# First graph layer of a fused graph and expert kernel: norms' squares summed on VectorE, early roots, and an aggregation that takes TH tile by tile for all banks

## The chip, the cores and the metric

One Trainium2 chip, one core. The metric is the device time of one execution, in microseconds; of several executions the median counts. TensorE is abbreviated PE (PEld for its weight loads), VectorE DVE, ScalarE ACT, GpSimd POOL, the engine that issues the DMAs SP.

## What is computed

Four blocks in a row, each added to its input: a hyperbolic graph convolution network of two layers on 625 nodes with 10,000 edges, a mixture of 8 experts, a plain graph network, and a linear attention block. The change lies in the first block, nearly all of it in its second layer. Cut to what matters:

```python
def gcn_conv(x, W, b, row, col, norm, n):
    h = mobius_matvec(W, x)         # mx = x @ W.T; needs |x| and |mx| of every row
    h = mobius_add(h, expmap0(b))   # needs the rows' dot products with the bias
    t = logmap0(h)                  # needs |h|, then artanh(|h|)
    msg = norm[:, None] * t[row]
    agg = jax.ops.segment_sum(msg, col, num_segments=n)
    return expmap0(agg)             # needs |agg|

def mobius_matvec(W, x):
    mx = x @ W.T
    xn, mxn = jnp.maximum(_norm(x), EPS), jnp.maximum(_norm(mx), EPS)
    res = jnp.tanh(mxn / xn * artanh(xn)) * mx / mxn
    return project(res)

x = x + _L0_gnn_ref(_layernorm(x, axis=-1), edge_index, ...)   # two gcn_conv
x = x + _L0_ffn_ref(_layernorm(x, axis=-1)[None], ...)[0]      # 8 experts, top 2
```

## The kernel before, in words

The 625 rows are five tiles (t = 0 to 4) of 125 partitions and 512 columns. The sum over edges is a matmul with a dense 625 x 625 count matrix, built from one-hot tiles (OHs, OHd) early in the kernel. A product of float32 accuracy is made from three single passes: each operand is split in a high part and a rest (CH and CL for the count matrix, TH and TL for the scaled messages, UH and UL for the aggregated features, W2H and W2L for the weights), and high x high, low x high and high x low are added up in a PSUM bank. PSUM has eight banks, PS[:, 0] to PS[:, 7], of 512 columns each.

Every engine has its own program, in the order in which it is written (`pe_gnn0`, `v_gnn0`, `a_gnn0`, `g_gnn0`, then the `..._moe` ones); engines wait for each other by counters only (`x.of(key)` is waited for, `x.up(key)` is counted up by the instruction that makes it). An engine whose next instruction waits does nothing behind it. The stages around the change, in order of time:

1. Aggregation of layer 0 (`pe_gnn0`, `share`, L914): for each of four feature blocks f and two halves h, a bank PS[2f+h] sums TH[k] x CH[k] over the five tiles k, then TL x CH, then TH x CL. ACT makes TH[k] one after the other (`a_scaled`, L486), DVE makes TL[k] (`v_scaled`, L492).
2. ACT copies the result of each f to UH and squares it to SQ[:, f]; DVE makes UL.
3. Token matmuls of layer 1 (`pe_token_matmul`, L822): twelve matmuls of 512 columns for each row tile t, in bank t. After t = 1 come the input norms: 20 matmuls of one column (4 blocks x 5 row tiles) of SQ with a column of ones, in bank 7 (`ss_mm`, L951).
4. The row step of layer 1: ACT squares each bank with its row sum (`a_rows`, L460, "ssm"), DVE multiplies it with the bias (`v_rows`, L342, "my"). POOL takes the square roots of ten columns at once, five of the input's norms (nu) and five of the product's (nm), when the last is there (L569). Then a chain of small instructions on DVE, five or ten columns wide: "rr" and "rcp" (the norms' reciprocals), "w" (from nu), "arg" (w x nm); Tanh on ACT; some twenty more up to "n2c" (L411); a root on POOL; then x, m, p, a polynomial, Ln on ACT, and the scale S. ACT meanwhile makes TT from the bias, DVE makes M[t] from bank t and TT[t] (`tangent`).
5. Aggregation of layer 1 (L952 to L962): PE waits for "n2c", runs 17 filler matmuls in bank 6 (`pe_busy`, results not used), and then for each row tile t takes 15 matmuls of 512 columns in bank t: CH x TH, CH x TL, CL x TH, five k each. Its waits are for M[t] and, before every k, for TL[k].
6. ACT squares each bank's result (JO), POOL takes the roots, DVE scales and adds into X. PE turns X (`ut_bank`, L1121) and makes the gate's logits; filler before that is in bank 6 (L1514). Routing follows, and then the experts' weight stream: SP loads a weight tile only when the matmuls that used its slot before are done (`w_used`, L1088). The first eight tiles are loaded long before.

## Time and profile before

| | us |
|---|---|
| median of 3 runs | 2160.74 (2158.61 to 2163.36) |
| profiled execution | 2158.04 |
| its span, first to last instruction | 2156.3 |
| TensorE busy in the span | 2096.2 (97%), 13312 matmuls |
| VectorE, ScalarE, GpSimd busy | 1491.4, 1119.2, 869.1 |
| stretch of the trace that the change touches | about 102 to 189 us |

The profile is of one execution. Its times are counted from the first instruction. The granted clock is the share of full speed that TensorE is given: 1.00 is 2.4 GHz, 0.50 is 1.2 GHz, and a value between them means that a window holds some of both. A matmul on float32 data that is not pre-split appears as two records, so the 20 norm matmuls are 40 rows. A window's count includes matmuls that only reach into it.

### The profile page before, as it was taken

To read this page: it belongs to the slowest core of one execution; us is meant where nothing else is said; L and a number is where in the kernel's file an instruction comes from. 1 tells how busy PE (TensorE), PEld (TensorE's weight loads), DVE (VectorE), ACT (ScalarE), POOL (GpSimd) and SP (SyncE) were. 2 spreads that over 40 slices of the span, in tenths; PEclk is the share of its full clock that TensorE was granted. 3 is DMA by queue.
4 is the path that set the end of the run, shared out by engine and by line. 5 is a ranking of instruction groups with operands and counts; after the bars stand their busy time and mean duration, and the time that the engine had idled before them with its cause. 6 is when DMAs were issued, how large, how long until landed. Compare 5 with 4: busy or idle time off the path is not lost.

```text
span 2156.3 us, 36026 instructions
## 1 busy us (share of the span) xinstructions
PE 2096.2 (97%) x13312; PEld 1956.7 (91%) x13312; DVE 1491.4 (69%) x3168; ACT 1119.2 (52%) x2999; POOL 869.1 (40%) x699
## 2 busy tenths in 40 slices
PE   8887999989999999999999999999999999999998
PEld 7766666677789999999999999999999999999997
DVE  8737988665366667767766677677666776776676
ACT  4534667624355455555554555555545555555464
POOL 0000000201165445555554555555545555555461
PEclk9888999999989999999999999999999999999999
DMA  6000899950131111123211111122111112221110
GB/s 215 1 28 11 301 333 332 272 188 1 34 120 63 63 63 63 63 65 107 81 63 63 63 63 63 65 104 83 63 63 63 63 63 66 106 81 63 60 45 24
DMA packets 89161, 201.15 MB, mean 93 GB/s; under 512 B 8196, under 2 KB 12580, under 8 KB 88985
## 3 DMA queue, kind: packets, MB, share of 16 engines
q1 hardware_dynamic: 86746, 196.28, 26.6%
q0 software_dynamic: 2240, 2.57, 0.5%
q8 instruction: 106, 1.74, 0.3%
q14 instruction: 69, 0.57, 0.1%
HBM read 196.31 MB, written 2.51 MB: 92 GB/s over the span
## 4 chain that ended last, share of the span: by engine, by line
PE 91%; DVE 4%; ACT 2%; DMA 1%; POOL 1%; issue 1%; SPq 0%; DVEq 0%; POOLq 0%; ACTq 0%
PE PS L54 82%; PE PS L53 5%; PE PS L57 4%; DMA YH<-y_rows,IH 1%; DMA X<-in_x 0%; DVE SM L107 0%; DVE OHs L68 0%; POOL SM L60 0%; DVE X L60 0%; POOL YL L125 0%; DVE OHd L69 0%; POOL YH L125 0%; ACT EE L88 0%; DVE JU L66 0%; DVE M L75 0%
## 5 line engine op out<-in xcount | busy, mean ns | idle before, releaser
L54 PE MATMUL PS<-ZH,WS 128*128 128x314 f32 x4096 | 946.5, 311 | 0.0
L54 PEld LDWEIGHTS PS<-ZH,WS 128*128 128x128 f32 x4096 | 692.2, 189 | 0.0
L54 PE MATMUL PS<-ZL,WS 128*128 128x314 f32 x2048 | 626.1, 306 | 0.0
L60 DVE TENSOR_TENSOR ACC<-ACC,PS 128x314 f32<-128x314 f32 x1008 | 476.6, 477 | 196.8 <-PE PS L54 186.8
L54 PEld LDWEIGHTS PS<-ZL,WS 128*128 128x128 f32 x2048 | 387.7, 189 | 0.0
L60 POOL TENSOR_TENSOR WS<-RAW,WS 128x512 fp32r<-128x512 f32 x256 | 326.1, 1294 | 117.0 <-ACT WS L88 117.0
L60 POOL TENSOR_TENSOR ZS<-ZS,ZQ 128x628 f32<-128x628 f32 x128 | 198.3, 1549 | 231.0 <-ACT ZQ L88 231.0
L60 POOL TENSOR_TENSOR ML<-MF,MH 128x400 fp32r<-128x400 f32 x124 | 130.7, 1054 | 364.5 <-ACT MH L88 364.5
L88 ACT ACTIVATE ZH<-PS,g1T 128x628 fp32r<-128x628 f32 x128 | 100.4, 785 | 313.8 <-PE PS L54 313.8
L88 ACT ACTIVATE EE<-EE,SM 125x100 f32<-125x100 f32 x640 | 233.0, 376 | 0.1
L88 ACT ACTIVATE MF<-PS 128x400 f32<-128x400 f32 x128 | 64.7, 505 | 315.9 <-PE PS L53 315.9
L75 DVE SCALAR_TENSOR_TENSOR ZL<-PS,g1T,ZH 128x628 fp32r<-128x628 f32 x128 | 111.6, 872 | 119.8 <-ACT ZQ L88 119.8
L60 POOL TENSOR_TENSOR WQ<-RAW,WQ 128x512 fp32r<-128x512 f32 x128 | 167.9, 1312 | 40.1 <-ACT WQ L88 40.1
L60 DVE TENSOR_TENSOR EE<-PS,CB 125x400 f32<-125x400 f32 x160 | 91.9, 575 | 132.3 <-PE PS L54 131.8
L60 DVE TENSOR_TENSOR EE<-EE,SM 125x500 f32<-125x500 f32 x128 | 153.6, 1200 | 4.4
L88 ACT ACTIVATE WS<-RAW 128x512 fp32r<-128x512 f32 x256 | 147.5, 633 | 0.0
L88 ACT ACTIVATE ATH<-PS 100x500 fp32r<-100x500 f32 (+1 forms) x256 | 96.4, 429 | 94.3 <-PE PS L57 94.3
L54 PE MATMUL PS<-MH,XH 128*125 128x400 f32 x640 | 144.2, 347 | 0.0
L54 PE MATMUL PS<-MH,XL 128*125 128x400 f32 x640 | 143.4, 346 | 0.0
L54 PE MATMUL PS<-ML,XH 128*125 128x400 f32 x640 | 142.9, 345 | 0.0
L53 PEld LDWEIGHTS PS<-KCL,WQ 128*128 128x128 f32 x1024 | 130.4, 192 | 2.2 <-issue 2.0
L53 PE MATMUL PS<-KCL,WQ 128*128 128x200 f32 (+1 forms) x1024 | 128.5, 268 | 0.8 <-DVE KCL L60 0.4
(354 smaller groups left out, 3565.3 us busy)
## 6 DMA issues: line engine op xcount, KB each, us to landing
RAW<-in_L_ffn_wz_w SPq DMA_DIRECT2D x66, 1024.0 KB, 5.9
RAW<-in_L_ffn_w SPq DMA_DIRECT2D x64, 1024.0 KB, 6.5
RAW<-in_L_ffn_Wq_w SPq DMA_DIRECT2D x32, 1024.0 KB, 8.6
CB<-c_rows SPq DMA_DIRECT2D x32, 195.3 KB
RAW<-in_L_gnn_W SPq DMA_DIRECT2D x4, 1024.0 KB, 15.9
RAW<-in_L_ffn_Wkv_w SPq DMA_DIRECT2D x4, 1024.0 KB, 15.2
RAW<-in_L_ffn_Wk_T SPq DMA_DIRECT2D x2, 1024.0 KB, 17.6
WB<-w_rows SPq DMA_DIRECT2D x6, 273.4 KB
```

Source lines behind the costliest of these rows:

```text
L53: return self.q.matmul(o, l, r, start=start, stop=stop, skip_group_check=True)
L54: return self.q.matmul(o, l, r, start=start, stop=stop)
L57: return Nothing() if self.q is None else self.q.transpose(o, i, idn)
L60: return Nothing() if self.q is None else self.q.tensor_tensor(out=o, in0=a, in1=b, op=op)
L75: return self.q.scalar_tensor_tensor(out=o, in0=a, scalar=s, in1=b, op0=op0, op1=op1)
L88: return self.q.activation(o, i, f, **kw)
```

## The change

- Aggregation of layer 0, blocks f = 0 and 1: the first pass (TH x CH) runs with k outside; each TH[k] is used for the four banks before the next is waited for. The number of matmuls stays.
- DVE adds SQ[:, 1], SQ[:, 2] and SQ[:, 3] into SQ[:, 0], after the four UL. The norms then take five matmuls instead of 20; they stand behind t = 2 instead of t = 1, and wait for the last sum. DVE copies them out one row tile earlier in its own order.
- POOL takes the roots in two instructions of five columns: nu as soon as it is there, nm behind the last square. DVE makes nu's reciprocal and "w" after "my" of tile 3; behind nm's roots stands "arg" at once, and nm's reciprocal (five columns instead of ten) behind that.
- ACT runs a Ln of one column right behind Tanh, whose result is not used.
- Aggregation of layer 1: the banks are 0, 1, 5, 6, 7 (`ag_bank`). The first pass (CH x TH) runs with k outside and waits for TH[k], not TL[k]; it also waits for M[1] and for the copy of the norms out of bank 7. Then 10 matmuls for each t.
- The gate's and the experts' banks are renumbered to fit (`ut_bank`, the mean term in bank 4, filler in bank 3, the table `free`).

```diff
@@ -361,18 +361,28 @@
                 else:
                     q.wait_ge(*row_a.of(1, "ssm", t))
                 step(q.stt(TT[:, t, :], rows_of_M(t), 1.0, Yk[:, :], ALU.mult, ALU.mult, acc=c["my"][:, t:t + 1]), ("my", t))
+                if k == 1 and t == 3:
+                    q.wait_ge(*row_g.of(1, "nu"))
+                    step(q.ts(ru, nu, EPS, None, ALU.max), "rru")
+                    after_("rru")
+                    step(q.rcp(ru, ru), "rcu")
+                    after_("rcu")
+                    step(q.stt(c["w"], ru, ATN, dis, ALU.mult, ALU.min), "w")
                 yield
             q.wait_ge(*row_g.of(k, "nn"))
-            step(q.ts(c["rr"], c["nn"], EPS, None, ALU.max), "rr")
-            after_("rr")
-            step(q.rcp(c["rr"], c["rr"]), "rcp")
-            after_("rcp")
             if k == 0:
+                step(q.ts(c["rr"], c["nn"], EPS, None, ALU.max), "rr")
+                after_("rr")
+                step(q.rcp(c["rr"], c["rr"]), "rcp")
+                after_("rcp")
                 step(q.ts(c["w"], ru, ATN, 1.0, ALU.mult, ALU.min), "w")
-            else:
-                step(q.stt(c["w"], ru, ATN, dis, ALU.mult, ALU.min), "w")
             after_("w")
             step(q.tt(c["w"], c["w"], nm, ALU.mult), "arg")
+            if k == 1:
+                step(q.ts(rm, nm, EPS, None, ALU.max), "rr")
+                after_("rr")
+                step(q.rcp(rm, rm), "rcp")
+                after_("rcp")
             yield
             q.wait_ge(*row_a.of(k, "r"))
             step(q.ts(c["r"], c["r"], MAXN, None, ALU.min), "r")
@@ -473,6 +483,8 @@
                 yield
             q.wait_ge(*row_v.of(k, "arg"))
             q.act(c["r"], c["w"], ACT.Tanh).then_inc(*row_a.up(k, "r"))
+            if k == 1:
+                q.act(R3["th"][:, 0:1], ones[0:P, 0:1], ACT.Ln).then_inc(*row_a.up("log"))
             yield
             for t in range(T5):
                 q.wait_ge(*row_v.of(k, "be"))
@@ -565,8 +577,9 @@
             q.wait_ge(*dis_v.of("deg"))
             g_power(q, dis, dis, hm[0:P, 0:5], row_g, "dis")
             q.wait_ge(*row_v.of(1, "ssu"))
+            g_power(q, R[1]["nn"][:, 0:5], R[1]["ss"][:, 0:5], hp[0:P, 0:5], row_g, 1, "nu")
             q.wait_ge(*row_a.of(1, "ssm", 4))
-            g_power(q, R[1]["nn"], R[1]["ss"], hp[0:P, 0:10], row_g, 1, "nn")
+            g_power(q, R[1]["nn"][:, 5:10], R[1]["ss"][:, 5:10], hp[0:P, 0:5], row_g, 1, "nn")
             q.wait_ge(*row_v.of(1, "n2c"))
             g_power(q, R[1]["n"], R[1]["n"], hp[0:P, 0:5], row_g, 1, "n")
             q.wait_ge(*row_a.of("out", "ss", 4))
@@ -656,7 +669,7 @@
             next(moe)
             for t in range(T5):
                 q.wait_ge(*ag_done.of(1, t))
-                q.act(JO[:, t, :], PS[0:P, t, :], ACT.Square, acc=R3["ss"][:, t:t + 1]).then_inc(*row_a.up("out", "ss", t))
+                q.act(JO[:, t, :], PS[0:P, ag_bank[t], :], ACT.Square, acc=R3["ss"][:, t:t + 1]).then_inc(*row_a.up("out", "ss", t))
             q.wait_ge(*row_v.of("out", "nd"))
             q.act(R3["th"], R3["nd"], ACT.Tanh).then_inc(*row_a.up("out", "th"))
             q.wait_ge(s_vec, 80)
@@ -789,8 +802,13 @@
             for f in range(4):
                 q.wait_ge(*u2_hi.of("u", f))
                 q.tt(halves(UL[:, f, :]), pair(f), halves(UH[:, f, :]).bitcast(f32), ALU.subtract).then_inc(*u2_lo.up(f))
+            for f in range(1, 4):
+                q.wait_ge(*u2_hi.of("sq", f))
+                if f >= 2:
+                    q.wait_ge(*u2_lo.of("sum", f - 1))
+                q.tt(SQ[:, 0, :], SQ[:, 0, :], SQ[:, f, :], ALU.add).then_inc(*u2_lo.up("sum", f))
             rows = v_rows(q, 1)
-            for t in range(4):
+            for t in range(3):
                 next(rows)
             q.wait_ge(*ss_mm.of())
             q.cp(R[1]["ss"][:, 0:5], PS[0:P, 7, 0:5]).then_inc(*row_v.up(1, "ssu"))
@@ -809,11 +827,13 @@
             q.stt(R3["cc"], R3["th"], MAXN, R3["rn"], ALU.min, ALU.mult).then_inc(*row_v.up("out", "cc"))
             q.wait_ge(*row_v.of("out", "cc"))
             for t in range(T5):
-                q.stt(X[:, t, :], PS[0:P, t, :], R3["cc"][:, t:t + 1], X[:, t, :], ALU.mult, ALU.add).then_inc(*x1_done.up(t))
+                q.stt(X[:, t, :], PS[0:P, ag_bank[t], :], R3["cc"][:, t:t + 1], X[:, t, :], ALU.mult, ALU.add).then_inc(*x1_done.up(t))
             q.wait_ge(s_vec, 80)
             for _ in moe:
                 pass
 
+
+        ag_bank = (0, 1, 5, 6, 7)
 
         def pe_busy(q, bank, tile, n):
             for _ in range(n):
@@ -923,10 +943,12 @@
             def tl(k):
                 return tl_done.of(0, k)
 
-            for f in range(2):
-                for h in range(2):
-                    q.wait_ge(*ch_done.of(4))
-                    share(f, h, TH, CH, True, False, th)
+            q.wait_ge(*ch_done.of(4))
+            for k in range(T5):
+                q.wait_ge(*th(k))
+                for f in range(2):
+                    for h in range(2):
+                        q.mm(PS[:, 2 * f + h, 0:HALF], TH[:, k, 128 * f:128 * f + 128], CH[:, k, HALF * h:HALF * h + HALF], k == 0, False)
             for f in range(2):
                 for h in range(2):
                     share(f, h, TL, CH, False, False, tl)
@@ -943,22 +965,24 @@
             for t in range(T5):
                 q.wait_ge(*u2_hi.of("sq", t // 2))
                 pe_token_matmul(q, 1, t, t)
-                if t == 1:
-                    q.wait_ge(*u2_hi.of("sq", 3))
+                if t == 2:
+                    q.wait_ge(*u2_lo.of("sum", 3))
                     for tt_ in range(T5):
-                        for k in range(4):
-                            i = q.mm(PS[0:P, 7, tt_:tt_ + 1], SQ[:, k, P * tt_:P * tt_ + P], ones[:, 0:1], k == 0, k == 3)
+                        i = q.mm(PS[0:P, 7, tt_:tt_ + 1], SQ[:, 0, P * tt_:P * tt_ + P], ones[:, 0:1], True, True)
                     i.then_inc(*ss_mm.up())
             q.wait_ge(*row_v.of(1, "n2c"))
             pe_busy(q, 6, W2H[:, 0, :], 17)
-            for t in range(T5):
-                q.wait_ge(*row_v.of(1, ("m", t)))
-                n = 0
-                for (l, r) in ((CH, TH), (CH, TL), (CL, TH)):
+            q.wait_ge(*row_v.of(1, ("m", 1)))
+            q.wait_ge(*row_v.of(1, "ssu"))
+            for k in range(T5):
+                q.wait_ge(*th_done.of(1, k))
+                for t in range(T5):
+                    q.mm(PS[0:P, ag_bank[t], :], CH[:, k, P * t:P * t + P], TH[:, k, :], k == 0, False)
+            for t in range(T5):
+                for (l, r) in ((CH, TL), (CL, TH)):
                     for k in range(T5):
                         q.wait_ge(*tl_done.of(1, k))
-                        i = q.mm(PS[0:P, t, :], l[:, k, P * t:P * t + P], r[:, k, :], n == 0, n == 14)
-                        n += 1
+                        i = q.mm(PS[0:P, ag_bank[t], :], l[:, k, P * t:P * t + P], r[:, k, :], False, l is CL and k == 4)
                 i.then_inc(*ag_done.up(1, t))
 
 
@@ -1118,7 +1142,7 @@
                 for t in range(T5):
                     q.gather(Y[:, t, :], yrow, index[:, t:t + 1]).then_inc(s_back, 16)
 
-        ut_bank = (5, 6, 0, 1, 3)
+        ut_bank = (3, 0, 1, 5, 6)
 
         def a_moe(q):
             def weights(i):
@@ -1270,7 +1294,7 @@
                 return ap.unsqueeze(2).broadcast_to([P, T5, 8])
 
 
-            q.tt(GS[:, :, :], b8(mean), PS[0:P, 7, 0:8].unsqueeze(1).broadcast_to([P, T5, 8]), ALU.mult).then_inc(*gate_v.up("mg"))
+            q.tt(GS[:, :, :], b8(mean), PS[0:P, 4, 0:8].unsqueeze(1).broadcast_to([P, T5, 8]), ALU.mult).then_inc(*gate_v.up("mg"))
             q.fill(rk[0][:, 0:1], 0.0)
             q.fill(rk[1][:, 0:1], 0.0).then_inc(*rank_v.up("zero"))
             q.wait_ge(*gate_pe.of("lg"))
@@ -1495,7 +1519,7 @@
             q.wait_ge(s_gw, 16)
             q.wait_ge(*row_v.of(1, "ssu"))
             for k in range(4):
-                i = q.mm(PS[0:P, 7, 0:8], ones[:, 0:P], gwT[:, k, :], k == 0, k == 3)
+                i = q.mm(PS[0:P, 4, 0:8], ones[:, 0:P], gwT[:, k, :], k == 0, k == 3)
             i.then_inc(*gate_pe.up("g"))
 
             def turned(t):
@@ -1511,7 +1535,7 @@
                 return i
 
             q.wait_ge(*w_hi.of(0, 1))
-            pe_busy(q, 6, HW[0], 13)
+            pe_busy(q, 3, HW[0], 13)
             turned(0)
             turned(1)
             turned(2)
@@ -1521,7 +1545,7 @@
                     turned(t + 3)
             i.then_inc(*gate_pe.up("lg"))
 
-            free = {0: mut_a.of(2), 1: mut_a.of(3), 2: gate_v.of("xg"), 3: mut_a.of(4), 4: x1_done.of(4), 5: mut_a.of(0), 6: mut_a.of(1), 7: gate_v.of("mg")}
+            free = {0: mut_a.of(1), 1: mut_a.of(2), 2: gate_v.of("xg"), 3: mut_a.of(0), 4: gate_v.of("mg"), 5: mut_a.of(3), 6: mut_a.of(4), 7: x1_done.of(4)}
 
             def rank_row(e):
                 q.wait_ge(*free[4])
```

## Rows read from the trace of the kernel before

**Rows 1.** The page's 40 slices: TensorE's granted clock, in tenths of full speed.
```profile
PEclk9888999999989999999999999999999999999999
```

**Rows 2.** Chain that ended last, 90 to 230 us: start, duration, engine, tile, line.
```profile
102.15 21.09 PE PS L54 x120
...
123.46 21.75 PE PS L54 x100
...
146.07 1.96 POOL SM L60
...
158.39 3.32 DVE TL L75 x5
```

**Rows 3.** TensorE's timeline, 100 to 112 us: start, duration, group, count, idle before it.
```profile
102.15 6.58 PE L54 MATMUL PS<-CH,TH 125*128 125x314 f32 x20 [2.61 <-ACT TH L88]
...
117.27 5.97 PE L54 MATMUL PS<-CL,TH 125*128 125x314 f32 x40
```

**Rows 4.** The weight loads' timeline (PEld) over the same first layer stretch.
```profile
104.50 3.97 PEld L54 LDWEIGHTS PS<-CH,TH 125*128 125x128 f32 x16 [0.32 <-ACT TH L88]
```

**Rows 5.** Windows: stretch, its length, busy time (count) per engine, granted clock, DMA.
```profile
102.15:108.40 6.25, 6.25 (x19) 5.01 (x20) 6.25 (x9) 4.20 (x6) 0.00 (x0) 0.52 0.01 3
...
132.20:134.65 2.45, 2.45 (x14) 2.45 (x13) 0.00 (x0) 0.00 (x0) 0.00 (x0) 0.50 0.00 0
134.65:138.90 4.25, 4.25 (x11) 3.35 (x12) 0.00 (x0) 0.00 (x0) 0.00 (x0) 0.50 0.00 0
139.46:142.27 2.81, 2.81 (x14) 2.23 (x13) 0.70 (x2) 0.69 (x2) 0.00 (x0) 1.00 0.00 0
...
152.10:155.90 3.80, 3.80 (x9) 2.59 (x10) 3.19 (x17) 3.42 (x6) 1.17 (x1) 0.50 0.00 0
...
161.75:178.30 16.55, 16.55 (x71) 13.25 (x72) 9.17 (x8) 10.22 (x16) 0.00 (x0) 1.00 0.00 1
182.30:189.00 6.70, 6.69 (x61) 6.30 (x59) 5.92 (x18) 2.83 (x5) 0.72 (x1) 1.00 0.02 4
```

**Rows 6.** TensorE's timeline, the norms and the filler before the second aggregation.
```profile
129.13 5.65 PE L54 MATMUL PS<-ones,SQ 128*125 128x1 f32 x40
...
152.09 5.96 PE L54 MATMUL PS<-W2H 128*94 128x512 f32 x17 [6.89 <-DVE SM L68]
```

**Rows 7.** VectorE's timeline, 92 to 200 us.
```profile
105.44 2.25 DVE L60 TENSOR_TENSOR CL<-CT,CH 125x628 fp32r<-125x628 f32 x3
...
124.00 0.81 DVE L60 TENSOR_TENSOR UL<-PS,UH 128x628 fp32r<-128x628 f32 x1 [0.64 <-ACT UH L88]
127.25 0.69 DVE L76 SCALAR_TENSOR_TENSOR TT<-PS,Y 125x512 f32<-125x512 f32 x1 [2.43 <-ACT M L88]
```

**Rows 8.** GpSimd's timeline, a square root of five columns.
```profile
152.11 1.17 POOL L60 TENSOR_TENSOR SM<-SM,hp 125x5 f32<-125x5 f32 x1 [4.09 <-DVE SM L68]
```

**Rows 9.** Chain that ended last, the small steps behind the norms, and a table load.
```profile
148.06 0.18 DVE SM L68
148.26 0.23 DVE SM L94
148.51 0.18 DVE SM L75
...
154.04 1.28 ACT L88
```

**Rows 10.** ScalarE's timeline, scaling into TH for the second aggregation.
```profile
156.44 3.17 ACT L88 ACTIVATE TH<-M,SM 125x512 fp32r<-125x512 f32 x5 [0.90 <-DVE SM L60]
```

**Rows 11.** Windows of TensorE alone: five banks in turn, then one bank at a time.
```profile
64.00:68.00 4.00, 4.00 (x32) 1.00 0.00 0
88.00:93.00 5.00, 5.00 (x39) 1.00 0.00 0
```

**Rows 12.** Windows: before the experts' weight stream, and in it; DMA share, GB/s last.
```profile
117.00:189.00 72.00, 63.13 (x317) 51.06 (x315) 35.90 (x96) 33.22 (x57) 5.00 (x4) 0.91 0.00 1
...
220.00:430.00 210.00, 209.93 (x941) 134.06 (x940) 172.79 (x372) 141.49 (x271) 13.68 (x10) 1.00 0.93 315
```

## Prediction, made before the changed kernel was run

> **What bounds the kernel now.** I read the chain that ended last first, in the stretch of the change [rows 2]. TensorE's matmuls carry the aggregation of layer 0 (21.09 us from 102.15) and the token matmuls with the norms (21.75 us from 123.46); then a row chain of small steps on POOL, DVE and ACT until the last TL is written at 158.39 + 3.32 = 161.71; then TensorE again. So in three of the four parts TensorE's own work and order set the end, and in the row part the number of dependent steps does. The page's line of the granted clock shows tenths below 9 in the slices in question, about 54 us each [rows 1], and the windows show where: 0.52 in the first pass of layer 0, 0.50 from 132.2 to 138.9, 0.50 in most of the filler [rows 5]. Behind this stretch, the DMA engines are idle until the experts' stream (share 0.00 from 117 to 189 us) and then at 0.93 with TensorE busy 209.93 of 210 us [rows 12]; whether a gain survives depends on what starts that stream.
>
> **Part 1, first pass of layer 0, k outside.** Today 20 matmuls go through one bank after the other. The first five follow ACT's TH tiles: the fifth weight load stands at 104.50, behind a wait for ACT, and from there 16 loads take 3.97 us, 0.25 us each, at the low clock [rows 4]. The pass ends near 104.50 + 3.97 = 108.4. With k outside, TH[0] feeds four matmuls, 4 x 0.25 = 1.0 us, more than the 0.6 us in which ACT makes the next tile (the five loads start 102.15 to 104.50, 0.59 us apart [rows 3, 4]), so the pass is no longer paced by ACT. All at the low clock it ends at 102.15 + 20 x 0.25 = 107.15, a gain of 1.2. At full clock a matmul of this shape takes 5.97 / 40 = 0.149 us [rows 3]. The clock rose today about 3.7 us after the dense run began at 104.50 (0.52 over the window to 108.4 [rows 5]); a run dense from 102.15 should see it earlier. If it comes as early as 104.5, nine matmuls are slow and eleven take 1.6: end 106.1, gain 2.3. I take the middle, **1.7 us** (1.2 to 2.3). TL x CH behind it finds its TL tiles (DVE writes them at 0.66 each from 102.1, the last before CL at 105.44 [rows 7]), the last CL is there at 105.44 + 2.25 = 107.7, and its consumers come ten us later. UH, UL, SQ and the second layer's start hang on this pass's end and move with it.
>
> **Part 2, norms.** Removed: 40 records of one column, 129.13 to 134.65 = 5.52 us on the path [rows 6, 5]. Their cost at full clock is (40 - 14) / (132.2 - 129.13), 0.12 us each, and 0.18 at the low one (2.45 us for 14 [rows 5]). Ten remain: 1.2 us, 1.8 at the low clock. The clock fell inside today's run, at about 132.2, and stayed low to 138.9: the token matmuls from 134.65 paid for it. A row tile of twelve takes 2.81 us at full clock; t = 2 ran 134.65 to 139.46 = 4.81 [rows 5]. That excess of 2.0 us goes too if a light run of 1.2 us doesn't bring the clock down. For this stands the gate's stretch, 182.3 to 189.0, in which light and dense matmuls alternate for 6.7 us at 1.00 [rows 5]. Sum: 5.5 - 1.2 + 2.0 = **6.3 us**; at the worst (ten at the low clock, the excess stays) 5.5 - 1.8 = 3.7.
>
> Added on DVE: three additions of 128x628. None of this kind (float32 from SBUF, in place) is in the trace; the nearest rows are CL, 2.25 / 3 = 0.75 us, and UL from PSUM, 0.81 [rows 7]. They follow UL[3], 124.00 + 0.81 = 124.81, one behind the other: done at 127.1 to 127.3. DVE's next step, "my" of tile 0, starts at 127.25 today [rows 7], so it is at most 0.1 us late, and "my" of tile 1 has 2.8 us per row tile to catch up. On PE the norms now stand behind t = 2, that is at 123.5 + 3 x 2.8 = 131.9, over 4 us after the last sum: no wait there. What is queued behind that wait are the token matmuls of t = 3 and 4; without the cover each late us would cost one. The norms' copy on DVE now waits for PE 1.2 us behind t = 2, while ACT's square and "my" of t = 2 take 1.5 us anyway. So the adds cost nothing.
>
> **Part 3, roots and row chain.** Behind the last square POOL takes 1.96 us for ten columns [rows 2], 1.17 for five [rows 8]: 0.8 gained. The other five run while PE is in t = 3 and 4. Behind the roots come today rr at 148.06, rcp 148.26, w 148.51, and arg from 148.71 [rows 9], 0.65 us before arg; now arg comes at once. The two instructions for nm's reciprocal run behind arg, where DVE waits 0.3 us for Tanh today; they need about 0.45, which costs 0.05. Gain 0.6. The new early part (max, reciprocal, w) lies behind "my" of t = 3, where DVE has over a us free. Sum **1.4 us** (1.2 to 1.5). Tanh's table load must be over by then: it starts behind the last square and takes 1.28 us, as the one of Ln does [rows 9], root and arg take about 1.5. The Ln placed behind Tanh loads its table (1.28) and runs (0.2) while DVE goes through the chain to "be", some 1.7 us; TT would start on time, and the load at 154.04 goes off the path, where DVE waited 0.37 us for Ln. This makes TH and TL 0.4 us earlier, and by part 4 they are not what comes last: priced at **0**, between 0 and 0.4.
>
> **Part 4, second aggregation.** Today 71 of the 75 matmuls come behind the last TL, from 161.75, at 16.55 / 71 = 0.233 us each [rows 5]; four more had been done in the waits, so the stage begins as if at 160.8. The filler, from "n2c" at 152.09, ends at 158.05 [rows 6]. In the new order 25 matmuls need TH[k] alone. TH[0] is ready at 156.44 + 0.63, less the 0.4 of the early Ln, 156.7 [rows 10], and the next follow at 0.63 against 5 x 0.233 = 1.17 us of work for each. So the start is set by the filler, 158.05; TL is needed 25 x 0.233 = 5.8 us later, 163.9, and is there by 161.7. Gain 160.8 - 158.05 = **2.8 us**. The filler's length is now on the path, and its clock with it: at the low clock throughout (3.80 us for 9 [rows 5]) it takes 7.2 us, end 159.3, gain 1.5; all at full clock it takes 4.0, then TH[0] decides at 156.8, gain 4.0. What is late next is CL, long there, and ACT's JO squares: its eight copies to HW follow the last TL and end near 169.5, JO[0] is ready at 163.9 + 2.3 = 166.2, and a square takes 0.8 against 2.3 per tile, so ACT has caught up by t = 2. The renumbered banks change no order; each bank's reader has long read it when it is written anew. No DMA and no queue of SP is moved; the one load that is released in this stretch waits for DVE's W2L, which stays where it is.
>
> **Sum.** 1.7 + 6.3 + 1.4 + 2.8 = 12.2 us. From 2158.04, the profiled execution, this gives 2145.8. The median of the three runs is 2.7 above it: 2160.74 - 12.2 = **2148.5**. Bounds of the terms: 1.2 + 3.7 + 1.2 + 1.5 = 7.6 and 2.3 + 6.3 + 1.5 + 4.0 = 14.1. The gain survives behind the stretch because the experts' weight tiles are loaded by `w_used`, that is by TensorE's own progress, and the first eight lie in SBUF long before; nothing in the trace is tied to an absolute time.
>
> **Rivals.**
> (a) *The clock falls behind the norms all the same.* In the new place they are the only light stretch in 14 us of token matmuls, but it may be enough. Then the excess of 2.0 us stays, and more if the ten run slow: gain 12.2 - 2.0 to 2.6, 2150.5 to 2151. Against it: the gate's stretch [rows 5].
> (b) *Interleaved banks cost TensorE.* 20 + 25 matmuls now change bank every time. If that slowed TensorE to its low clock in the second aggregation, a matmul would take 0.42 (the filler) instead of 0.233: 75 x 0.19 = 14 us more, so 2160.7 - 12.2 + 14 = 2163, slower than before. It decides from 12.2 / 0.19, 64 of the 75 matmuls. Against it: the one-hot matmuls go through five banks in turn at 32 in 4 us at clock 1.00, 0.125 each, and those that stay in one bank 39 in 5 us, 0.128 [rows 11]. The Trainium skill, "TensorE: Matmul & The Clock Gate", section "A second HAM failure mode: psum-queue depth-cycling", tells of a kernel whose cycling through banks let TensorE idle briefly between groups, so that its clock swung between both levels; by that rule this rival would hold, and the trace here does not agree.
> (c) *The experts' stream gives it back.* With the DMA share at 0.93 the stream may be what bounds that phase. If its start did not move, all 12.2 us would be lost there: 2160. Against it: share 0.00 until TensorE frees the first slot.
> (d) *It does not do what it says*: PE waits at the norms for DVE's sums, if an addition took 2.5 us instead of 0.8. Then some 5 us of part 2 go back: about 2153. The rows of this size on DVE speak against it.
>
> **How the numbers follow.** Forecast 2148.5, chance 0.72; (a) 0.12, 2150.7; (b) 0.04, 2163; (c) 0.06, 2160; (d) 0.03, 2153; 0.03 for something that I don't see, on either side. The range holds the term bounds and some of the medians' own uncertainty (the runs before lie within 2.6 us of theirs): 2160.7 - 14.1 - 1.6 = 2145.0 to 2160.7 - 7.6 + 0.4 = 2153.5, which takes in (a) and (d). A measurement of this kernel tells about 0.2%, 4.3 us, from no change: faster 0.90 (forecast, a, d and part of the rest), same 0.06, slower 0.04.
>
> **What would show it.** In the new trace: the first TH x CH group is dense from its start and about 5 us long; the group of ones and SQ has 10 records over about 1.2 us, with the granted clock 1.00 through t = 3 and 4; POOL has two roots of five columns, arg follows the second at once; a table load stands right behind Tanh; the second aggregation starts right behind the filler and its 75 matmuls take 17.5 us. Right if the gate's first turn comes 12 us earlier and the shift is the same at the first expert's matmuls and at the end. Wrong if the clock is 0.50 behind the norms (a) or in the interleaved pass (b), or if the shift shrinks between 200 and 430 us (c).

## The result

| | kernel before | changed kernel |
|---|---|---|
| median (15 runs each) | 2160.94 us (2155.88 to 2165.01) | 2149.24 us (2143.44 to 2157.41) |
| profiled execution's span | 2156.3 us | 2144.5 us |
| TensorE busy | 2096.2 us | 2088.0 us |

The ratio is 0.9946, with a 95% interval from 0.9933 to 0.9958: 11.7 us less, and the interval excludes 1. Beside the last experiments the same pair gave 2161.13 (14 runs) and 2151.45 us (9 runs), ratio 0.9958, 0.9942 to 0.9974. 2148.5 had been predicted.

### The profile page after: what moved, and what is told of

It is laid out like the page before. It is cut to its first block, busy times and chain, and to the rows that moved or that the text cites. A ratio compares the mean times of both kernels' runs of the same rounds, so it can differ in the third digit from the quotient of the medians.

```text
span 2144.5 us, 35976 instructions
## 1 busy us (share of the span) xinstructions
PE 2088.0 (97%) x13282; PEld 1950.4 (91%) x13282; DVE 1494.2 (70%) x3173; ACT 1121.4 (52%) x3000; POOL 870.8 (41%) x700
## 4 chain that ended last, share of the span: by engine, by line
PE 92%; DVE 4%; DMA 1%; POOL 1%; ACT 1%; issue 1%; SPq 0%; DVEq 0%; POOLq 0%; ACTq 0%
PE PS L54 82%; PE PS L53 5%; PE PS L57 4%; DMA YH<-y_rows,IH 1%; DMA X<-in_x 0%; DVE SM L107 0%; POOL SM L60 0%; DVE X L60 0%; POOL YL L125 0%; DVE OHs L68 0%; POOL YH L125 0%; DVE JU L66 0%; DVE OHd L69 0%; DVE SM L60 0%; ACT EE L88 0%
## 6 DMA issues: line engine op xcount, KB each, us to landing
RAW<-in_L_ffn_Wk_T SPq DMA_DIRECT2D x2, 1024.0 KB, 17.6
```

## The profile after

The page of the changed kernel: TensorE (busy, share of the span, instructions), and the granted clock in 40 slices, which answers to [rows 1].

```profile
PE 2088.0 (97%) x13282; PEld 1950.4 (91%) x13282; DVE 1494.2 (70%) x3173; ACT 1121.4 (52%) x3000; POOL 870.8 (41%) x700
...
PEclk9898999989999999999999999999999999999999
```

The chain that ended last (start, duration, what), the pieces that answer to [rows 2]. The first aggregation takes 19.08 us where it took 21.09, the token matmuls with the norms 15.35 where it was 21.75, POOL's root 1.18 for 1.96, and the piece with VectorE's TL has gone from the chain: TensorE runs from the filler to the last result without a gap, 23.51 us.

```profile
102.84 19.08 PE PS L54 x120
...
122.15 15.35 PE PS L54 x70
...
138.29 1.18 POOL SM L60
...
142.94 23.51 PE PS L54 x92
```

TensorE's timeline (start, duration, group, count). From the first TH x CH matmul to the first TL x CH it is 107.26 - 102.84 = 4.42 us, where it was 6.42; the norms are 10 records in 1.15 us for 40 in 5.65 [rows 6]; the second aggregation begins right behind the filler, and its first pass, 25 matmuls, takes 154.63 - 148.81 = 5.82 us.

```profile
102.84 4.58 PE L54 MATMUL PS<-CH,TH 125*128 125x314 f32 x20 [2.62 <-ACT TH L88]
107.26 3.05 PE L54 MATMUL PS<-CH,TL 125*128 125x314 f32 x20
...
130.67 1.15 PE L54 MATMUL PS<-ones,SQ 128*125 128x1 f32 x10
...
142.94 6.03 PE L54 MATMUL PS<-W2H 128*94 128x512 f32 x17 [5.45 <-DVE SM L68]
148.81 5.99 PE L54 MATMUL PS<-TH,CH 125*125 125x512 f32 x25
154.63 1.33 PE L54 MATMUL PS<-TL,CH 125*125 125x512 f32 x5
```

Windows of the same trace (length, busy time and count of PE, PEld, DVE, ACT, POOL, then granted clock, DMA). The clock is 1.00 in and behind the norms and in the pass that changes bank with every matmul. The last two rows are of the routing, which the change does not touch: TensorE does nothing for 3 us, still granted the full clock, and the dispatch behind it gets 0.63.

```profile
130.67:131.68 1.01, 1.01 (x12) 1.01 (x10) 0.09 (x1) 0.69 (x2) 0.00 (x0) 1.00 0.00 0
131.68:137.50 5.82, 5.80 (x26) 4.34 (x25) 1.82 (x8) 0.69 (x2) 1.17 (x1) 1.00 0.00 0
148.81:154.60 5.79, 5.79 (x26) 4.63 (x25) 4.61 (x8) 3.63 (x6) 0.00 (x0) 1.00 0.00 0
...
191.80:194.80 3.00, 0.07 (x1) 0.00 (x0) 2.89 (x17) 0.00 (x0) 0.00 (x0) 1.00 0.00 1
194.84:204.00 9.16, 7.72 (x29) 5.91 (x29) 3.64 (x12) 1.52 (x3) 0.00 (x0) 0.63 0.10 32
```

VectorE's timeline: three additions in 2.64 us; "my" of tile 0 begins as the last one ends, 3.83 us behind the first token matmul (3.79 before); at 139.49 "arg" follows the roots at once.

```profile
123.42 2.64 DVE L60 TENSOR_TENSOR SQ<-SQ 128x628 f32<-128x628 f32 x3
125.98 0.68 DVE L76 SCALAR_TENSOR_TENSOR TT<-PS,Y 125x512 f32<-125x512 f32 x1
...
139.49 0.17 DVE L60 TENSOR_TENSOR SM<-SM 125x5 f32<-125x5 f32 x1 [0.55 <-POOL SM L60]
```

ScalarE's timeline: the table load for Ln, now right behind Tanh, and TH.

```profile
139.91 1.28 ACT L88 ACT_TABLE_LOAD   x1
...
146.96 3.18 ACT L88 ACTIVATE TH<-M,SM 125x512 fp32r<-125x512 f32 x5 [1.75 <-DVE SM L60]
```

To compare parts, the trace is divided at instructions that every kernel here has. (A) the first pass of layer 0, from its first matmul to the first TL one; (B) from the first token matmul to the start of ScalarE's last square; (C) from there to the filler's start; (D) from there to the start of ScalarE's last JO square, with the filler's length up to the first aggregation matmul in brackets; (E) from there to the first expert matmul. Each row is one profiled execution; all numbers are us and differences of starts in its timelines.

| kernel | A | B | C | D (filler) | E |
|---|---|---|---|---|---|
| before | 6.42 | 21.78 | 6.85 | 26.47 | 34.57 |
| changed | 4.42 | 15.37 | 5.42 | 23.53 (5.87) | 37.77 |
| changed, second profile (e12_after_again) | 4.67 | 15.38 | 5.40 | 23.68 (6.03) | 34.63 |
| e1_norms20 | 5.37 | 20.23 | 5.40 | 23.61 (5.97) | 37.81 |
| e2_norms5_early | 4.54 | 15.33 | 5.41 | 23.63 (5.97) | 37.80 |
| e3_k_out_tl | 4.26 | 15.37 | 5.41 | 24.49 (5.95, then a wait) | 34.63 |
| e4_t_out_th | 5.37 | 15.37 | 5.41 | 24.20 (6.58) | 38.84 |
| e5_t_out_tl | 5.37 | 15.37 | 5.42 | 26.15 | 34.63 |
| e6_roots_late | 4.69 | 15.38 | 6.85 | 22.99 (5.36) | 37.51 |
| e7_ln_late | 5.30 | 15.37 | 5.41 | 23.99 (6.34) | 38.84 |
| e8_layer0_bank | 6.62 | 15.38 | 5.41 | 24.01 (6.35) | 38.84 |
| e9_fill13 | 5.34 | 15.37 | 5.41 | 23.14 (5.47) | 35.30 |
| e10_l0_route | 3.21 | 15.37 | 5.40 | 24.42 (6.76) | 35.70 |
| e11_combo | 4.24 | 15.38 | 5.40 | 22.61 (4.89) | 36.10 |

Between the two profiled executions A to D give 2.00 + 6.41 + 1.43 + 2.94 = 12.78 us; the changed one had begun A 0.69 later, and lost 3.20 in E. The first expert matmul is 213.13 - 204.24 = 8.89 us earlier, and the spans differ by 11.8: the rest came back further down, where nothing was changed. From the first expert matmul to the end the fourteen profiles have 1939.7 to 1944.0 us (span less that matmul's start), so differences of 2 to 4 us in a total say nothing of a part; the parts are judged by the stretches A to E. One place at which time came back lies at about 540 us, in 40 matmuls that are the same in both kernels: those of the kernel before ended at a clock of 0.72 (546.0 to 550.5 us), those of the changed one at 1.00 (536.4 to 540.9 us), and that alone is 1.4 us. The first row is of the kernel before, the second of the changed one.

```profile
542.06 7.78 PE L53 MATMUL PS<-Wp,fU 125*128 125x100 f32 x40 [0.48 <-DVE Wp L75]
532.49 6.34 PE L53 MATMUL PS<-Wp,fU 125*128 125x100 f32 x40 [0.48 <-DVE Wp L75]
```

## Experiments

All start from the changed kernel and undo or alter one thing. Where not said otherwise they were run once, with a profile; what is compared is the stretch that the edit touches.

### The norms: is it the number, the place, or the clock?

**e1_norms20**: 20 matmuls again, at the new place, no sums.

```diff
-            for f in range(1, 4):
-                ...
-                q.tt(SQ[:, 0, :], SQ[:, 0, :], SQ[:, f, :], ALU.add).then_inc(*u2_lo.up("sum", f))
...
                 if t == 2:
-                    q.wait_ge(*u2_lo.of("sum", 3))
+                    q.wait_ge(*u2_hi.of("sq", 3))
                     for tt_ in range(T5):
-                        i = q.mm(PS[0:P, 7, tt_:tt_ + 1], SQ[:, 0, P * tt_:P * tt_ + P], ones[:, 0:1], True, True)
+                        for k in range(4):
+                            i = q.mm(PS[0:P, 7, tt_:tt_ + 1], SQ[:, k, P * tt_:P * tt_ + P], ones[:, 0:1], k == 0, k == 3)
```

> The changed kernel without DVE's sums: the norms are again 20 matmuls (40 records), at the new place behind t = 2. Measured from the first token matmul to the end of the last one: 15.4 us in the changed kernel. Theory (the length of the one-column run costs twice, by itself and by the clock that falls in it and stays low behind it): the 40 records take 4.7 to 5.5 us instead of 1.15, the granted clock reaches 0.50 in or right behind them, the row tile behind takes up to 4.8 instead of 2.8, the stretch is 20.5 to 21.8 us. Rival (the clock fell before for another reason, as the place behind t = 1): clock 1.00 throughout, stretch 15.4 + 3.5 = 18.9.

Its timeline of TensorE, the norms and the first group behind them:

```profile
131.68 4.42 PE L54 MATMUL PS<-ones,SQ 128*125 128x1 f32 x40
135.96 1.62 PE L54 MATMUL PS<-W2H,UH 128*125 128x512 f32 x3
```

Its windows: the first 3.1 us of the norms, the row tile t = 3 behind them, and t = 4.

```profile
131.68:134.80 3.12, 3.12 (x31) 3.12 (x29) 0.70 (x2) 0.69 (x2) 0.00 (x0) 1.00 0.00 0
...
135.96:139.70 3.74, 3.74 (x12) 2.96 (x12) 0.17 (x1) 0.00 (x0) 1.17 (x1) 0.54 0.00 0
140.40:143.20 2.80, 2.80 (x13) 2.04 (x11) 1.14 (x5) 0.69 (x2) 0.00 (x0) 1.00 0.00 0
```

TensorE is busy all through, and the clock is still 1.00 in the norms, but t = 3 behind them gets 0.54. B is 20.23 us, 4.9 more than with five matmuls: 3.3 of it the records themselves (4.28 us to the next group, 1.01 with five matmuls), the other 1.6 the slow row tile. It is a little below the range expected, since the clock fell only behind the norms here; before the change it fell within them, and B was 21.78. The rival, that the old place was to blame, falls. Another row says the same of one-column matmuls: the 25 degree matmuls ahead of layer 0 (`ones`, CT, 50 records) keep TensorE busy without a gap in all 14 profiles, and in all 14 the granted clock falls to 0.50 before they end.

**e2_norms5_early**: the five matmuls at the old place.

```diff
-                if t == 2:
+                if t == 1:
                     q.wait_ge(*u2_lo.of("sum", 3))
```

> The changed kernel with the five norm matmuls at the old place, behind t = 1. Theory (the place is worth nothing, only the number): the last sum is done 3.9 us after the token matmuls begin, t = 1 ends at 5.6, so no wait; the stretch is 15.4 us as in the changed kernel, clock 1.00. Rival (the later place hides the sums): the matmuls wait for the sums, the stretch grows by the wait and more if the clock falls, 16 us or more.

B is 15.33 us, against 15.37: the place is worth nothing. The sums are done well before either: the last ends 3.9 us behind the first token matmul, and t = 1 at 5.6.

### The second aggregation: the wait or the order?

The part has two halves, the order (k outside) and the wait (TH[k] for TL[k]). Three kernels with the remaining combinations of them in the first pass:

```diff
 # e3_k_out_tl
             for k in range(T5):
-                q.wait_ge(*th_done.of(1, k))
+                q.wait_ge(*tl_done.of(1, k))
                 for t in range(T5):
 # e4_t_out_th
-            for k in range(T5):
-                q.wait_ge(*th_done.of(1, k))
-                for t in range(T5):
+            for t in range(T5):
+                for k in range(T5):
+                    q.wait_ge(*th_done.of(1, k))
 # e5_t_out_tl: as e4, with tl_done
```

> The changed kernel, but the first pass of the second aggregation waits for TL[k] instead of TH[k]; k stays outside. From the filler's start to the last aggregation matmul's end: 23.4 us in the changed kernel. Theory (either half of this part alone does nearly all): it starts at TL[0], 0.7 us behind the filler's end, and is then not paced, since 5 x 0.233 = 1.17 us per k is more than TL's 0.66: 24.1 us. Rival (the earlier wait bought the whole part): 23.4 + 2.9 = 26.3 us.

Its timeline of TensorE: the pass begins 6.77 us behind the start of the filler, after a wait of 0.82 us for the first TL, and has no other.

```profile
148.92 6.04 PE L54 MATMUL PS<-TH,CH 125*125 125x512 f32 x25 [0.82 <-DVE TL L75]
```

D is 24.49 us, 0.96 more than the changed kernel's profile, of which 0.82 is the wait. The rival's 2.9 falls. What the wait costs depends on the filler: it took 5.95 us here. Behind one of 6.76 us (e10 below, D 24.42) TL[0], 6.77 us behind the filler's start, would be there as it ends; that is worked out from these rows and was not run.

> The changed kernel, but the first pass of the second aggregation has the row tile t outside and k inside, one bank at a time; the wait is for TH[k] as in the change. Theory (the order of k matters little once the wait is for TH): the fifth matmul waits for TH[4], some 0.4 us, then all is there: 23.8 us from the filler's start, and its 25 matmuls run at 0.233 us each as the interleaved ones do. Rival 1 (the order k outside bought the part): 26 us. Rival 2 (changing the bank every matmul costs TensorE something): the pass is shorter than the interleaved one's 5.8 us, apart from the wait.

```profile
146.75 6.75 PE L54 MATMUL PS<-W2H 128*94 128x512 f32 x17 [5.44 <-DVE SM L68]
153.33 5.95 PE L54 MATMUL PS<-TH,CH 125*125 125x512 f32 x25
159.12 1.31 PE L54 MATMUL PS<-TL,CH 125*125 125x512 f32 x5
```

The filler took 6.58 us here (granted clock 0.57, 0.65 in the changed kernel's) and covered even the wait for TH[4]; behind the filler D has 24.20 - 6.58 = 17.62 us, against 23.53 - 5.87 = 17.66 with k outside. The pass one bank at a time takes 159.12 - 153.33 = 5.79 us, the interleaved one 5.82: changing the bank with every matmul costs nothing that can be seen. Behind a filler of 5.87 us this order would not have been free: TH[4] is done 7.20 us behind the filler's start (146.96 + 3.18 - 142.94 in the changed kernel), the fifth matmul would stand at 5.87 + 4 x 0.233 = 6.80, and the wait, as an estimate from these rows, would be 0.4 us.

> The changed kernel with both halves of the second aggregation's first pass undone: row tile outside, k inside, wait for TL[k]. Each half alone left 24.5 us (k outside, wait for TL) and 24.2 us (t outside, wait for TH, of which 0.7 is a longer filler) from the filler's start to the last square of the result, 23.5 in the changed kernel. Theory (the two are substitutes: the loss comes only when the fifth matmul needs the last TL): TL[4] is done 9.3 us behind the filler's start, four matmuls are done by then, 71 x 0.233 = 16.6 us follow: 26.0 us. Rival (the losses add up): 23.5 + 1.0 + 0 to 0.7 = 24.5 to 25.2 us.

Its timeline: two matmuls start the pass, and the next ones come one by one as each TL appears.

```profile
153.26 1.06 PE L54 MATMUL PS<-TH,CH 125*125 125x512 f32 x2
154.49 0.50 PE L54 MATMUL PS<-TH,CH 125*125 125x512 f32 x1 [0.17 <-DVE TL L75]
155.16 0.49 PE L54 MATMUL PS<-TH,CH 125*125 125x512 f32 x1 [0.17 <-DVE TL L75]
```

D is 26.15 us, the 26.0 of the theory, and 0.32 below the kernel before (26.47): the first aggregation matmul stands 6.77 us behind the filler's start, where it was 7.10, which fits the 0.33 us of the early Ln (e7 below). So the two halves are substitutes, not addends. Undone alone, one costs nothing behind its long filler (e4) and the other 1.0 us (e3); both together cost 2.6 (26.15 less the changed kernel's 23.53). The large loss comes only when one bank's first five matmuls need the last TL.

### The row chain

**e6_roots_late**: one root of ten columns, and max, reciprocal and w behind it.

```diff
-                if k == 1 and t == 3:
-                    ...
-                    step(q.stt(c["w"], ru, ATN, dis, ALU.mult, ALU.min), "w")
...
+            step(q.ts(c["rr"], c["nn"], EPS, None, ALU.max), "rr")
...
+            step(q.rcp(c["rr"], c["rr"]), "rcp")
...
+            step(q.stt(c["w"], ru, ATN, dis, ALU.mult, ALU.min), "w")
...
-            g_power(q, R[1]["nn"][:, 0:5], R[1]["ss"][:, 0:5], hp[0:P, 0:5], row_g, 1, "nu")
-            g_power(q, R[1]["nn"][:, 5:10], R[1]["ss"][:, 5:10], hp[0:P, 0:5], row_g, 1, "nn")
+            g_power(q, R[1]["nn"], R[1]["ss"], hp[0:P, 0:10], row_g, 1, "nn")
```

> The changed kernel with the roots of ten columns in one instruction behind the last square and max, reciprocal and w behind them, as before the change. From the start of the last square to the filler's first matmul: 5.42 us in the changed kernel, 6.85 in the one before. Theory: 6.8 us, of which 0.8 is POOL's instruction (1.95 instead of 1.17). Rival (ACT's table load sets the time of Tanh anyway): below 6.4.

C is 6.85 us, the kernel before's to the hundredth. Its VectorE timeline has the ten-column steps ahead of "arg" (141.04) again, the first two here; POOL's root of ten columns takes 1.95 us.

```profile
140.38 0.17 DVE L68 TENSOR_SCALAR SM<-SM 125x10 f32<-125x10 f32 x1 [1.40 <-POOL SM L60]
140.59 0.22 DVE L94 RECIPROCAL SM<-SM 125x10 f32<-125x10 f32 x1
```

**e7_ln_late**: without the Ln behind Tanh.

```diff
-            if k == 1:
-                q.act(R3["th"][:, 0:1], ones[0:P, 0:1], ACT.Ln).then_inc(*row_a.up("log"))
```

> The changed kernel without the Ln behind Tanh. Theory (the filler sets the start of the second aggregation): the first TH is 0.4 us later against the filler's start, the table load stands again behind the TT copies, but the stretch from the filler's start to the last square of the result stays at 23.5 us plus what the filler's own clock changes. Rival (TH[0] sets it): 23.9 us, with idle time behind the filler.

ScalarE's table load stands behind the TT copies again, and TH follows at 150.63, 4.35 us behind the filler's start (4.02 in the changed kernel):

```profile
148.23 1.28 ACT L88 ACT_TABLE_LOAD   x1
...
150.63 3.18 ACT L88 ACTIVATE TH<-M,SM 125x512 fp32r<-125x512 f32 x5 [0.90 <-DVE SM L60]
```

TensorE goes from the filler to the aggregation with no idle time between them all the same:

```profile
146.28 6.51 PE L54 MATMUL PS<-W2H 128*94 128x512 f32 x17 [5.45 <-DVE SM L68]
152.62 5.97 PE L54 MATMUL PS<-TH,CH 125*125 125x512 f32 x25
```

Behind the filler D has 23.99 - 6.34 = 17.65 us. The early Ln is worth 0.33 us to TH and nothing to the kernel, as long as the filler stands where it does; where the pass waits for TL, as in e5, it shows.

### The first pass of layer 0

**e8_layer0_bank**: one bank at a time.

```diff
-            for k in range(T5):
-                q.wait_ge(*th(k))
-                for f in range(2):
-                    for h in range(2):
-                        q.mm(PS[:, 2 * f + h, 0:HALF], TH[:, k, ...], CH[:, k, ...], k == 0, False)
+            for f in range(2):
+                for h in range(2):
+                    share(f, h, TH, CH, True, False, th)
```

> The changed kernel with the first pass of layer 0 one bank at a time again. From its first matmul to the first TL matmul: 6.42 us in the kernel before, 4.42 in the changed one, 4.26 to 5.37 in four runs that keep the new order. Theory (ACT's TH tiles pace the first five matmuls, and the clock rises later): 5.8 to 6.9 us, with idle time between the first five. Rival (the clock's moment alone made the difference): it falls among the four others.

Its weight loads (PEld), the first four each behind a wait for ScalarE, as before the change:

```profile
102.85 0.29 PEld L54 LDWEIGHTS PS<-CH,TH 125*128 125x128 f32 x1 [0.26 <-ACT TH L88]
103.46 0.29 PEld L54 LDWEIGHTS PS<-CH,TH 125*128 125x128 f32 x1 [0.33 <-ACT TH L88]
104.07 0.29 PEld L54 LDWEIGHTS PS<-CH,TH 125*128 125x128 f32 x1 [0.33 <-ACT TH L88]
104.69 4.17 PEld L54 LDWEIGHTS PS<-CH,TH 125*128 125x128 f32 x16 [0.33 <-ACT TH L88]
```

A is 6.62 us. The ten profiles with the new order and no added filler have 4.26 to 5.37, 4.93 in the mean; the old order has 6.42 and 6.62. They don't overlap, so it is not the clock's moment alone (the moment at which the granted clock rises in that execution), though that moment spreads the new order's values over 1.1 us. The matmuls' starts tell the two apart. At the low clock they are 0.26 us apart. In e8 all but the first five are, and the pass takes 6.62 us; in five profiles of the new order (e1, e4, e5, e7, e9) all are, or all but the last, and it takes 5.30 to 5.37. So ACT's pace cost 1.3 us. In the other five the clock rises within the pass, behind the 10th to 15th matmul, which takes off 0.6 to 1.1 us more.

### What the filler costs and what it could still bring

**e9_fill13**: 13 filler matmuls in place of 17 before the second aggregation.

> The changed kernel with 13 filler matmuls before the second aggregation instead of 17. In the profiles so far the 17 took 5.36 to 6.58 us, and the aggregation began right behind them, while TH[0] is ready about 4.7 us behind the filler's start. Theory (the filler's last matmuls lie on the path): the stretch from the filler's start to the last square is 0.9 us shorter, 22.1 to 23.3 us. Rival (the filler is what keeps the clock up for the aggregation): the 25 matmuls behind it take over 6.3 us instead of 5.8, and the stretch is 23.4 us or more.

```profile
146.50 5.64 PE L54 MATMUL PS<-W2H 128*94 128x512 f32 x13 [5.44 <-DVE SM L68]
151.97 6.00 PE L54 MATMUL PS<-TH,CH 125*125 125x512 f32 x25
```

The filler takes 5.47 us for 13, nearly all at the low clock; with 17 it took 5.36 to 6.76. The 25 matmuls behind it take 157.81 - 151.97 = 5.84 us, so the rival falls. D is 23.14, within the range expected, but so is one kernel with 17 (22.99): between single profiles the clock's moment moves D by 1.4 us, more than the four matmuls do. That the filler lies on the path is shown by D less the filler, which is 17.6 to 17.7 in all kernels in which the aggregation follows at once; the mean gain was not measured.

**e10_l0_route** and **e11_combo**: filler where TensorE has nothing to do. e11 has the 13 too.

```diff
+            pe_busy(q, 6, UH[:, 0, :], 6)
             q.wait_ge(*ch_done.of(4))
             for k in range(T5):
                 q.wait_ge(*th(k))
...
-            pe_busy(q, 2, HW[0], 14)
+            pe_busy(q, 2, HW[0], 20)
```

> The changed kernel with two more pieces of filler: six matmuls of 512 columns between the degree matmuls and the wait for layer 0's first TH, and 20 instead of 14 before the first dispatch. Theory (both stretches run at the low clock because TensorE does little or nothing ahead of them, and the filler costs nothing because it fits the wait): the first pass of layer 0 takes 3.0 to 4.3 us instead of 4.3 to 5.4, and from the last square of the aggregation to the first expert matmul it is 34.6 to 35.3 us instead of the 37.5 to 38.8 of most runs of the new order. Rival (the moment of the clock's changes is chance, filler or not): first pass 4.3 to 5.4, last stretch 37.5 or more.

e10's timeline of TensorE around the first filler, and its windows of layer 0's first pass, of the gate's last 24 small matmuls and of the dispatch:

```profile
99.78 2.85 PE L54 MATMUL PS<-UH 128*94 128x512 f32 x6
102.53 3.37 PE L54 MATMUL PS<-CH,TH 125*128 125x314 f32 x20
```

```profile
102.53:105.70 3.17, 3.17 (x21) 3.17 (x21) 3.17 (x5) 3.17 (x6) 0.00 (x0) 0.92 0.02 5
...
173.62:177.60 3.98, 3.98 (x26) 3.91 (x24) 1.87 (x12) 0.59 (x1) 1.98 (x6) 0.64 0.00 0
195.26:199.30 4.04, 4.04 (x25) 3.18 (x25) 2.94 (x10) 0.59 (x1) 0.00 (x0) 1.00 0.23 74
```

Layer 0's first pass takes 3.21 us, the lowest of all; in e11 it is 4.24, no more than the best without filler (4.26). The dispatch runs at clock 1.00, in e10 and in e11, where the changed kernel's profile had 0.63. Two profiles alone would not show that the filler did it, since some without it have 1.00 too, but all fourteen together do so better. The dispatch starts 6.5 us behind the first matmul of the filler ahead of it in every one of them, however long that filler takes. In five the idle time left between them is 1.2 to 1.6 us: in e10 and e11 by the 20 matmuls, in before, e9 and e12 because the 14 ran partly at the low clock. All five take 6.3 us from the dispatch's first matmul to the first expert one. In nine it is 3.0 us: seven of these take 8.9 to 9.4, and e3 and e5 take 6.3.

E as a whole, 35.7 and 36.1 us, misses the range expected (34.6 to 35.3) all the same: the gate's last 24 small matmuls, 2.7 us at clock 1.00, took 4.0 and 4.4. They lie ahead of the added filler. These matmuls lost the clock in e4, e7, e8 and e9 too, which have no filler added there, and the three profiles with an E of 38.84 are those that lost the clock in both places. So the theory holds for the dispatch (filler in a wait keeps the clock up for what follows); for the gate the filler does nothing.

> The changed kernel with all three filler edits: six before layer 0's aggregation, 13 instead of 17 before the second one, 20 instead of 14 before the first dispatch. Theory: about 1.2 + 0.9 + 2 = 4 us below the changed kernel of the same call, that is some 16 us below the one before, ratio 0.9925. Rival (chance): the same as the changed kernel, 0.9946.

> The changed kernel itself, unedited, beside the one with three filler edits on the same chip. Expected 11.7 us below the kernel before (0.9946), with the first pass of layer 0 between 4.3 and 5.4 us, and the stretch to the first expert matmul either 34.6 or 37.5 to 38.8 us.

The changed kernel's second profile lies in both ranges expected, A 4.67 and E 34.63 us; its median is 9.7 us below the kernel before, where 11.7 was expected. Run beside one another: before 2161.13 us (14 runs), changed 2151.45 (9 runs), all three filler edits 2146.52 (6 runs), ratio to before 0.9932 (0.9918 to 0.9946) against 0.9958 (0.9942 to 0.9974) for the change alone. The medians of e11 and e12 differ by 4.9 us, about the 4 expected; the intervals still overlap, from 0.9942 to 0.9946. The edited kernel is probably the faster of the two; by how much is not settled.

## Why the prediction was right

- **Part 1**, priced 1.7 (1.2 to 2.3): 2.00 between the two profiles; 1.6 in the mean (the two of the old order, 6.52, less 4.93). Both halves of the mechanism are seen: ACT's pace, 1.3 us by e8 against the five passes at the low clock, and the rise within the pass, 0.6 to 1.1 us, but that in half of the profiles only. Where it came, it came behind ten to fifteen matmuls; nine had been assumed.
- **Part 2**, 6.3 (3.7 to 6.3): 6.41. Its three terms: the records, 5.52 less 1.01 to the next group = 4.5 where 4.3 was reckoned; the slow row tile, 4.81 less 2.87 = 1.9 where 2.0 was; and no wait for the sums. (The quotient for a record at full clock stands upside down in the prediction; 3.07 us / 26 is the 0.12 that it goes on with.) The adds took 2.64 us where 2.3 to 2.4 was assumed, and delayed nothing. e1 shows that the second term belongs to the number of matmuls, e2 that the new place brings nothing.
- **Part 3**, 1.4 (1.2 to 1.5): 1.43, and 1.44 when undone (e6).
- **The early Ln**, 0: right (e7). The prediction named the filler as what decides, and it does.
- **Part 4**, 2.8 (1.5 to 4.0): 2.94; the nine profiles with 17 fillers in which the aggregation begins right behind them have 22.99 to 24.42 us in D, 2.1 to 3.5 below the 26.47, as the filler's clock has it. The prediction put the part on both halves together; e3 and e4 show that either alone gives more than half or all of it.
- **Rivals.** (a) the clock falling behind five matmuls: not seen in any of the 12 profiles that have them, all with a B of 15.33 to 15.38. (b) interleaving: 5.82 against 5.79 us, clock 1.00. Here the row [rows 11] decided rightly. The rule that the prediction names beside it, the Trainium skill's "TensorE: Matmul & The Clock Gate", section "A second HAM failure mode: psum-queue depth-cycling", tells of short idle times between groups; in the interleaved pass TensorE was busy for 5.79 of 5.79 us, so no run here shows what such idle times would do. (c) the stream gives it back: the shift was 8.89 us at the first expert matmul (213.13 before) and 8.82 at the last matmul of the same group, 211 us later, so nothing was lost in the stream. (d) the wait for the sums: none.
- **What the sum did not hold, and luck.** 12.2 was predicted, 12.78 stands in the stretches A to D, and 11.7 and 9.7 were measured. That the first of these came out so close is partly luck: of the 11.8 us between the two spans, 3.2 had been lost in E and 2.9 came back behind it, both in code that the change does not touch. The stretch E, in which nothing was changed, took 34.6 us in the profile of before and 37.8 in that of after. The prediction took such a shift to be constant behind the change ("the shift is the same at the first expert's matmuls and at the end"), and that was wrong: it was 12.1 us at the last square, 8.9 at the first expert and 11.8 at the end. Of the eleven profiles from the changed kernel on that have 14 fillers there, three have 34.63, e9 35.30, and seven 37.5 to 38.8.

The two rows of the kernel before that answer to the last two of the changed kernel's windows above: here the filler ran partly at the low clock, so it ended later, the idle time before the dispatch was 1.4 us instead of 3, and the dispatch got 1.00.

```profile
205.40:206.80 1.40, 0.01 (x1) 0.00 (x0) 1.33 (x9) 0.00 (x0) 0.00 (x0) 1.00 0.01 2
206.86:211.00 4.14, 4.08 (x25) 3.18 (x25) 2.96 (x11) 0.59 (x1) 0.00 (x0) 1.00 0.31 72
```

Whether this happens more often after the change than before is open: there is one profile of before, and e3 and e5 had 3 us of idle time at this place too and kept the clock. It may be why the changed kernel's runs spread over 14 us (2143.4 to 2157.4) and those of before over 9.

## What to carry to other kernels

A long run of matmuls with one column cost twice on TensorE here: its own time, and the clock of the dense work behind it. Forty records (4.3 and 5.5 us) did so in both profiles that have them, ten (1.0 us) in none of twelve. Sum on an engine that waits anyway, and keep such runs short. When a pass waits for its operands one by one, let it wait for the part that it uses, or spread it over several banks so that no matmul needs the last operand early; either alone left 0 to 1 us here, by the filler's length. Filler that keeps the clock up lies on the path as soon as the work behind it is ready, so it has to be measured again when a change makes that work ready earlier.

## What the runs showed that was not expected

- TensorE busy without a gap is not enough for the full clock. In e1 40 one-column records at 100% busy ended in a stretch at 0.54. The gate's 24 matmuls of eight columns, again without idle time, kept the clock in eight profiles (2.7 to 2.9 us, the kernel before and the changed one among them) and lost it in six (3.6 to 4.5 us; 0.64 and 0.58 in e10 and e11). The prediction had taken that stretch as the evidence that light work alternating with dense work is safe [rows 5]; it was right for 1.15 us of norms and too generous for the gate.
- Three microseconds without any matmul were followed by a dispatch that lost the clock in seven profiles (0.63 in the changed kernel), and by one at full clock in two (e3, e5). Identical code therefore has stretches that differ by 3 to 4 us from one execution to the next.
- A stretch ahead of the change has two lengths as well: the first TH x CH matmul comes at 102.2 to 102.8 us in nine of the profiles and at 104.8 to 105.5 in the other five, in kernels that are the same up to there but for e10's and e11's filler. Most of it lies in the degree matmuls ahead, 50 one-column records again: they take 5.6 to 6.2 us in the nine and 7.8 to 8.3 in the five (e4, e5, e7, e9, e11). In the nine the clock falls 4.6 to 5.3 us behind their start, in the five 2.4 to 2.9 us; at 97 to 98 us it is 1.00 in the changed kernel and 0.50 in e7. Why it falls sooner in some executions stays open. The rows are of the changed kernel and of e7.

```profile
94.30 5.93 PE L53 MATMUL PS<-ones,CT 125*125 125x1 f32 x50
94.44 8.26 PE L53 MATMUL PS<-ones,CT 125*125 125x1 f32 x50
```
